# First layer's weighted sums: rows by group of 512 edges instead of by step

## The chip, the cores and the metric

One core of a Trainium2 chip runs the whole program. The metric is the device time in microseconds of one execution, as the median of several runs.

## What is computed

The reference is a stack of four graph layers on 6,250 nodes and 206,250 edges, which arrive sorted by their target node `dst`. Each layer's result is added to `x` and normalised. The change touches the first layer alone, an attention layer with 8 heads of 16 columns:

```
e   = leaky(score_src[src] + score_dst[dst] + edge_bias)      # one number per edge and head
p   = exp(e - max over the edges with the same dst)
msg = x_heads[src] * edge_gate                                # 128 numbers per edge
out = segment_sum(msg * p, dst) / segment_sum(p, dst)         # per node and head
```

The last line is the part at issue: per node, the sum over its edges of the 128-wide row times the edge's weight, and the sum of the weights.

## The kernel before

The program runs its stages one after the other, with a barrier between two stages. Earlier stages have written the gated rows `x_heads[src] * edge_gate` to HBM (`gated`) and hold the weights `p` in `e_score`. `stage_aggregate` (L811) then makes the two segment sums, and `stage_update` divides and normalises.

Edges lie in tiles of 128, four tiles make a group (G = 4, 512 edges), and there are GE = 403 groups. Nodes lie in 49 blocks of 128. Since edges are sorted by node, a group touches one block or a few; the stage runs over pairs of a group and a block in order, called steps: KE = 451 steps, 48 more than groups. The table `steps_e`, made on the device by `stage_steps` (L282), says for step k which group (row 0) and which block (row 1) it has; its row 2 is the group modulo 8 (SLOTS), its row 3 the number of steps that are through when a group is through. Rows 2 and 3 are used by a later stage, `stage_move`, too.

In each step, in rings of R = 8 buffers:

- SyncE loads the group's gated rows into `ag_buf` (L831), 256 KB.
- GpSimd multiplies them by the weights into columns 0 to 127 of `ag_wrow` (L835), and ScalarE copies the 8 weights of each edge into the 8 columns behind them (L898). Both may write a buffer when TensorE is through with the step 8 back (`s_mm`).
- VectorE makes the one-hot matrix `ag_oh`, 128 edges by 128 nodes for each of the four tiles, by comparing a count with the keys (L872, SCALAR_TENSOR_TENSOR).
- TensorE multiplies one-hot by weighted rows, four float32 matmuls that add up in one of four PSUM tiles (L912). Each float32 matmul stands in the trace as two.
- VectorE adds the PSUM tile to the block's rows of `acc` (L885, TENSOR_TENSOR), three steps later.

Every engine works through its own list of instructions in order. `pipeline` (L159) writes the loops: 8 steps in a turn of the loop, so that buffer numbers are constants, and a few steps ahead and behind it written out.

Of the kernel before, what the change touches and what calls it, by code (L numbers as in the profile page):

```python
# [19 lines left out]
ALU = mybir.AluOpType  # L20
# [5 lines left out]
ds = bass.ds  # L26

P = 128
C = 128
# [6 lines left out]
G = 4  # L36
# [11 lines left out]
SLOTS = 8  # L48
# [134 lines left out]
def later(item, by=RING):  # L183

    return not isinstance(item, int) or item >= by
# [13 lines left out]
def flat(ap):  # L199
    return ap.rearrange("p a c -> p (a c)")  # L200

def stage_node_table(nc, v, name, rhs, table, scores, loads=(), kept=W):

    R = 4
    s_x, s_t, s_xt, s_h, s_row, s_sc = (v.sem(f"{name}_{n}") for n in ("x", "t", "xt", "h", "row", "sc"))
    s_st = [v.sem(f"{name}_st{u}") for u in range(R)]
    with ExitStack() as mem:  # L210
# [152 lines left out]
def step_value(nc, eng, steps, row, k, top):  # L363

    _, values = nc.values_load_multi_w_load_instructions(  # L365
        steps[0:1, row, ds(k, 1)], engines=[eng.engine], min_val=0, max_val=top, skip_runtime_bounds_check_because=SURE)
    return values[0]
# [443 lines left out]
def stage_aggregate(nc, v, name, rows, keys, steps, n_steps, groups, weights, heads, acc):  # L811

    R = 8
    s_z, s_ld, s_oh = v.sem(name + "_z"), [v.sem(f"{name}_ld{u}") for u in range(R)], v.sem(name + "_oh")
    s_w, s_wc, s_mm, s_add = v.sem(name + "_w"), v.sem(name + "_wc"), v.sem(name + "_mm"), v.sem(name + "_add")
    s_up = v.sem(name + "_up")
    width = C + heads
    with ExitStack() as mem:
        sb = lambda n, sh, d=F32: mem.enter_context(nc.sbuf_tensor(name + n, sh, d))  # L820
        buf = sb("_buf", [P, R, G, C])
        oh = sb("_oh", [P, R, G, P])
        wrow = sb("_wrow", [P, R, G, width])
        ps = [mem.enter_context(nc.psum_tensor(f"{name}_ps{u}", [P, 512], F32)) for u in range(4)]
        count_up = mem.enter_context(nc.psum_tensor(name + "_up", [P, 512], F32))
        src = rows.rearrange("(t p) c -> p t c", p=P)
        with nc.Block() as block:
            def load(queue, k, u, g):
                if later(k, R):
                    queue.wait_ge(s_w, k - R + 1)  # L830
                queue.dma_start(buf[:, u, :, :], src[:, ds(g * G, G), 0:C]).then_inc(s_ld[u], 16)  # L831

            def weigh(engine, queue, k, u, use, g):
                queue.wait_ge(s_ld[u], use * 16 + 16)
                engine.tensor_tensor(  # L835
                    wrow[:, u, :, 0:C].rearrange("p t (h c) -> p t h c", h=heads),
                    buf[:, u, :, :].rearrange("p t (h c) -> p t h c", h=heads),
                    weights[:, ds(g * G, G), 0:heads][:, :, :, None].broadcast_to([P, G, heads, C // heads]),
                    ALU.mult).then_inc(s_w, 1)

            @block.sync
            def _(sp):
                def loads(k, u, use):
                    g = step_value(nc, sp, steps, 0, k, groups - 1)
                    load(sp, k, u, g)

                pipeline(sp, n_steps, (loads, 0), ring=R)

            @block.gpsimd  # L850
            def _(pool):
                def weighted(k, u, use):
                    g = step_value(nc, pool, steps, 0, k, groups - 1)
                    if later(k, R):
                        pool.wait_ge(s_mm, k - R + 1)
                    weigh(nc.gpsimd, pool, k, u, use, g)

                pipeline(pool, n_steps, (weighted, 0), ring=R)

            @block.vector  # L860
            def _(dve):
                nc.vector.memset(acc[:, :, 0:width], 0.0).then_inc(s_z, 1)
                nc.vector.tensor_copy(count_up[:, 0:P], v.iota[:, :]).then_inc(s_up, 1)
                dve.wait_ge(s_up, 1)

                blocks = Blocks(nc, dve, steps, groups, 3, R)

                def prepare(k, u, use):
                    g, b = blocks.load(k, u)
                    if later(k, R):  # L870
                        dve.wait_ge(s_mm, k - R + 1)
                    nc.vector.scalar_tensor_tensor(  # L872
                        oh[:, u, :, :], count_up[:, None, 0:P].broadcast_to([P, G, P]), v.blk[:, ds(b, 1)],
                        keys[:, ds(g * G, G), None].broadcast_to([P, G, P]), ALU.add,
                        ALU.is_equal).then_inc(s_oh, 1)

                def add(k, u, use):
                    b = blocks.again(k, u)
                    dve.wait_ge(s_mm, k + 1)
                    if later(k, 1):  # L880
                        dve.wait_ge(s_add, k)
                    else:
                        dve.wait_ge(s_z, 1)
                    here = flat(acc[:, ds(b, 1), 0:width])
                    nc.vector.tensor_tensor(here, here, ps[u % 4][:, 0:width], ALU.add).then_inc(s_add, 1)  # L885

                pipeline(dve, n_steps, (prepare, 0), (add, 3), ring=R)

            @block.scalar
            def _(act):  # L890
                nc.scalar.preload_act_table(ACT.Copy)

                def put(k, u, use):
                    g = step_value(nc, act, steps, 0, k, groups - 1)
                    if later(k, R):
                        act.wait_ge(s_mm, k - R + 1)
                        act.wait_ge(s_z, 1)
                    nc.scalar.activation(wrow[:, u, :, C:width], weights[:, ds(g * G, G), 0:heads],  # L898
                                         ACT.Copy).then_inc(s_wc, 1)

                pipeline(act, n_steps, (put, 0), ring=R)

            @block.tensor
            def _(pe):
                def sums(k, u, use):
                    pe.wait_ge(s_oh, k + 1)
                    pe.wait_ge(s_w, k + 1)
                    pe.wait_ge(s_wc, k + 1)
                    if later(k, 4):
                        pe.wait_ge(s_add, k - 3)  # L910
                    for j in range(G):
                        last = nc.tensor.matmul(ps[u % 4][:, 0:width], oh[:, u, j, :], wrow[:, u, j, 0:width],  # L912
                                                start=(j == 0), stop=(j == G - 1))
                    last.then_inc(s_mm, 1)

                pipeline(pe, n_steps, (sums, 0), ring=R)
# [1438 lines left out]
```

## Time and profile before

| what | value |
| --- | --- |
| median of 3 runs | 9192.17 us |
| the runs | 9183.11 to 9197.33 us |
| the profiled execution, first to last instruction | 9188.8 us |
| mean granted TensorE clock | 0.886 |
| the stage that is changed | 2574 to 3141 us of the span |

The profile is one execution, the median is over three others. What lies around the span isn't given by itself; the span is 3.4 us under the median and within the spread of the runs. Engines work beside each other, so busy times don't add up to the span. An engine's sequencer isn't counted as busy.

### The profile page before, as it was taken

The numbers are of one execution on the slowest core, as the hardware profiler recorded it, in microseconds if no ns is written. First come the engines' busy times: TensorE is split into PE (matmuls) and PEld (weight loads), VectorE is DVE, ScalarE is ACT, GpSimd is POOL, SyncE is SP. The second block draws the span as 40 slices with busy tenths as digits, with TensorE's granted clock in tenths as the row PEclk, the third lists the DMA queues.
The fourth block names the chain that finished last, engine by engine and source line by source line (L and its number), as shares of the span: only waits on it lengthen the run. The fifth ranks groups of instructions, "written<-read, shape, count | busy, mean of one in ns | idle before, by whom it ended". The sixth has DMA issues, their size and how long they took to land. (4 is left out here: it accounts for less than half of the span.)

```text
span 9188.8 us, 193747 instructions
## 1 busy us (share of the span) xinstructions
PE 6564.0 (71%) x41828; PEld 5489.2 (60%) x41829; DVE 6345.2 (69%) x11929; ACT 1632.9 (18%) x4649; POOL 6369.9 (69%) x7772
## 2 busy tenths in 40 slices
PE   5999999999378548777777625999768850037752
PEld 3878877888267536666666524777558740026652
DVE  3444444444577868777777524888768899999965
ACT  1111111110221134444444200111410000011100
POOL 2777777775068557777777764888367778877774
PEclk9999999999789879999999857999889975569975
DMA  3777777777067436666666769999359963359974
GB/s 115 207 206 208 208 207 206 209 207 200 24 177 210 128 113 211 209 208 209 209 209 208 213 172 157 273 270 270 103 163 264 259 188 86 87 159 256 253 210 115
DMA packets 2113959, 1742.97 MB, mean 190 GB/s; under 512 B 376688, under 2 KB 1838118, under 8 KB 2113686
## 3 DMA queue, kind: packets, MB, share of 16 engines
q1 hardware_dynamic: 1217548, 819.30, 30.4%
q10 hardware_dynamic: 710140, 472.87, 20.6%
q0 software_dynamic: 186160, 449.72, 17.3%
q14 instruction: 90, 0.74, 0.0%
q8 instruction: 21, 0.34, 0.0%
HBM read 1289.62 MB, written 453.29 MB: 190 GB/s over the span
## 5 line engine op out<-in xcount | busy, mean ns | idle before, releaser
L1592 POOL DMA_INDIRECT z_xg<-table,srci x1664 | 1819.1, 1093 | 512.9 <-issue 466.3
L1162 POOL DMA_INDIRECT sorted<-m_rows,srci x1612 | 1609.0, 998 | 532.4 <-issue 436.1
L464 POOL DMA_INDIRECT g_xg<-table,srci x1612 | 1582.1, 981 | 491.2 <-issue 464.3
L1458 PE MATMUL n_ps<-n_row,n_oh 128*128 128x257 f32 x3712 | 881.2, 389 | 216.0 <-DVE n_row L1434 198.1
L483 PE MATMUL g_psg<-g_wg,g_eT 128*128 128x136 f32 x3224 | 1027.6, 474 | 0.0
L1458 PEld LDWEIGHTS n_ps<-n_row,n_oh 128*128 128x128 f32 x3712 | 677.6, 190 | 419.5 <-issue 337.4
L500 PE MATMUL g_psx<-scores,g_hot 128*128 x3608 | 835.5, 362 | 70.3 <-DVE e_score L591 68.0
L483 PEld LDWEIGHTS g_psg<-g_wg,g_eT 128*128 128x128 f32 x3224 | 769.3, 324 | 191.0 <-issue 191.0
L500 PEld LDWEIGHTS g_psx<-scores,g_hot 128*128 128x128 f32 x3608 | 806.8, 329 | 86.9 <-issue 85.9
L1656 PE MATMUL z_ps<-z_wrow,z_oh 128*128 128x132 f32 x3712 | 603.4, 315 | 329.8 <-issue 188.8
L564 DVE TENSOR_TENSOR g_y<-g_gate,g_xg 128x512 f32<-128x512 f32 x403 | 279.7, 694 | 787.5 <-DMA g_xg<-table,srci 786.8
L835 POOL TENSOR_TENSOR ag_wrow<-ag_buf,e_score 128x512 f32<-128x512 f32 x451 | 467.3, 1057 | 438.8 <-DMA ag_buf<-gated 350.0
L1656 PEld LDWEIGHTS z_ps<-z_wrow,z_oh 128*128 128x128 f32 x3712 | 521.5, 216 | 411.5 <-issue 374.4
L1221 PE MATMUL m_psx<-held,m_hot 128*128 x3608 | 599.1, 316 | 192.8 <-DVE m_rows L1340 120.1
L1221 PEld LDWEIGHTS m_psx<-held,m_hot 128*128 128x128 f32 x3608 | 507.5, 217 | 253.4 <-issue 252.5
L1628 PE MATMUL z_ps<-z_tab,z_ohlo 128*128 128x200 bf16 x4992 | 600.7, 250 | 75.9 <-DVE z_e L1746 71.6
L1340 DVE SCALAR_TENSOR_TENSOR m_rows<-m_rows,follows,m_psx 128x516 f32 x451 | 339.4, 753 | 347.1 <-ACT m_rows L1266 287.3
L523 ACT ACTIVATE g_gate<-g_psg 128x512 f32<-128x512 f32 x403 | 240.6, 597 | 1833.4 <-PE g_psg L483 1752.9
L912 PE MATMUL ag_ps<-ag_wrow,ag_oh 128*128 128x136 f32 x3608 | 489.4, 289 | 80.9 <-DVE ag_oh L872 80.8
L1211 PE MATMUL m_psl<-m_cnt,m_oht 128*128 128x100 f32 x3224 | 542.9, 296 | 0.0
L912 PEld LDWEIGHTS ag_ps<-ag_wrow,ag_oh 128*128 128x128 f32 x3608 | 445.1, 190 | 125.2 <-issue 114.1
L1211 PEld LDWEIGHTS m_psl<-m_cnt,m_oht 128*128 128x128 f32 x3224 | 510.7, 200 | 1.2
(411 smaller groups left out, 12549.7 us busy)
## 6 DMA issues: line engine op xcount, KB each, us to landing
n_row<-sorted SPq DMA_DIRECT2D x464, 520.0 KB, 4.4
z_buf<-gathered ACTq DMA_DIRECT2D x464, 256.0 KB
g_keys<-dst_row ACTq DMA_DIRECT2D x451, 256.0 KB
ag_buf<-gated SPq DMA_DIRECT2D x451, 256.0 KB, 3.2
m_keys<-dst_row ACTq DMA_DIRECT2D x451, 256.0 KB
gathered<-z_xg SPq DMA_DIRECT2D x416, 256.0 KB
gated<-g_y SPq DMA_DIRECT2D x403, 256.0 KB
g_eT<-in_attr_t SPq DMA_DIRECT2D x402, 256.0 KB
```

What stands on the lines that cost most here:

```text
L464: nc.gpsimd.indirect_dma_start(out=xg[:, u, j, :], out_offset=None, in_=v.table[:, :], in_offset=bass.IndirectOffsetOnAxis(ap=v.srci[:, t: ...
L483: last = nc.tensor.matmul(psg[u % 2][:, h, j * W:(j + 1) * W], eT[:, u, (h * H + j) * P:(h * H + j + 1) * P], wg[:, :], start=False, stop= ...
L500: last = nc.tensor.matmul(psx[u % 2][:, j * X8:(j + 1) * X8], hot_t[:, u, j * P:(j + 1) * P], flat(v.scores[:, ds(b, 1), :]), start=True, ...
L835: engine.tensor_tensor(wrow[:, u, :, 0:C].rearrange("p t (h c) -> p t h c", h=heads), buf[:, u, :, :].rearrange("p t (h c) -> p t h c", h= ...
L912: last = nc.tensor.matmul(ps[u % 4][:, 0:width], oh[:, u, j, :], wrow[:, u, j, 0:width], start=(j == 0), stop=(j == G - 1))
L1162: nc.gpsimd.indirect_dma_start(out=v.sorted[:, :], out_offset=bass.IndirectOffsetOnAxis(ap=place[:, t:t + 1], axis=0), in_=rows[:, u, j, : ...
L1211: nc.tensor.matmul(to, oht[:, u, j * P:(j + 1) * P], before, start=True, stop=False)
L1221: last = nc.tensor.matmul(psx[u % 2][:, j // 2, (j % 2) * WH:(j % 2 + 1) * WH], hot_t[:, u, j * P:(j + 1) * P], flat(held[:, ds(b, 1), :]) ...
L1458: last = nc.tensor.matmul(ps[u % 4][:, 0:ROW], oh[:, u, j, :], row[:, u, j, 0:ROW], start=(j == 0), stop=(j == G - 1))
L1592: nc.gpsimd.indirect_dma_start(out=xg[:, u, j, :], out_offset=None, in_=v.table[:, :], in_offset=bass.IndirectOffsetOnAxis(ap=v.dsti[:, t: ...
L1628: nc.tensor.matmul(to, ohlo[:, u, edges], tab[:, n, :, :], start=(n == 0), stop=False)
L1656: last = nc.tensor.matmul(bank[u % 4 // 2][:, u % 2, 0:width], oh[:, u, j, :], wrow[:, u, j, 0:width], start=(j == 0), stop=(j == G - 1))
```

## The change

The steps stay, and so do VectorE's part and the order of the matmuls. SyncE, GpSimd and ScalarE now go over the 403 groups instead of the 451 steps. Group g has slot g modulo 8 in `ag_buf` and `ag_wrow`. SyncE may load group g when TensorE is through with the last step of group g - 8; it reads the number of that step from row 3 of the table and waits for the count `s_mm`. GpSimd and ScalarE wait for the load alone. TensorE has to find the slot: for each step it loads the group (row 0, with the bounds check, for the waits `s_w` and `s_wc`, which count groups now) and the slot (row 2), and the second operand of each matmul has an address worked out from the slot.

```diff
--- before.py
+++ after.py
@@ -811,7 +811,7 @@
 def stage_aggregate(nc, v, name, rows, keys, steps, n_steps, groups, weights, heads, acc):
 
 
-    R = 8
+    R = SLOTS
     s_z, s_ld, s_oh = v.sem(name + "_z"), [v.sem(f"{name}_ld{u}") for u in range(R)], v.sem(name + "_oh")
     s_w, s_wc, s_mm, s_add = v.sem(name + "_w"), v.sem(name + "_wc"), v.sem(name + "_mm"), v.sem(name + "_add")
     s_up = v.sem(name + "_up")
@@ -825,37 +825,27 @@
         count_up = mem.enter_context(nc.psum_tensor(name + "_up", [P, 512], F32))
         src = rows.rearrange("(t p) c -> p t c", p=P)
         with nc.Block() as block:
-            def load(queue, k, u, g):
-                if later(k, R):
-                    queue.wait_ge(s_w, k - R + 1)
-                queue.dma_start(buf[:, u, :, :], src[:, ds(g * G, G), 0:C]).then_inc(s_ld[u], 16)
-
-            def weigh(engine, queue, k, u, use, g):
-                queue.wait_ge(s_ld[u], use * 16 + 16)
-                engine.tensor_tensor(
-                    wrow[:, u, :, 0:C].rearrange("p t (h c) -> p t h c", h=heads),
-                    buf[:, u, :, :].rearrange("p t (h c) -> p t h c", h=heads),
-                    weights[:, ds(g * G, G), 0:heads][:, :, :, None].broadcast_to([P, G, heads, C // heads]),
-                    ALU.mult).then_inc(s_w, 1)
-
-
             @block.sync
             def _(sp):
-                def loads(k, u, use):
-                    g = step_value(nc, sp, steps, 0, k, groups - 1)
-                    load(sp, k, u, g)
-
-                pipeline(sp, n_steps, (loads, 0), ring=R)
+                def load(g, u, use):
+                    if later(g, R):
+                        done = sp.value_load(steps[0:1, 3, ds(g - R, 1)], min_val=1, max_val=n_steps)
+                        sp.wait_ge(s_mm, done)
+                    sp.dma_start(buf[:, u, :, :], src[:, ds(g * G, G), 0:C]).then_inc(s_ld[u], 16)
+
+                pipeline(sp, groups, (load, 0), ring=R)
 
             @block.gpsimd
             def _(pool):
-                def weighted(k, u, use):
-                    g = step_value(nc, pool, steps, 0, k, groups - 1)
-                    if later(k, R):
-                        pool.wait_ge(s_mm, k - R + 1)
-                    weigh(nc.gpsimd, pool, k, u, use, g)
-
-                pipeline(pool, n_steps, (weighted, 0), ring=R)
+                def weighted(g, u, use):
+                    pool.wait_ge(s_ld[u], use * 16 + 16)
+                    nc.gpsimd.tensor_tensor(
+                        wrow[:, u, :, 0:C].rearrange("p t (h c) -> p t h c", h=heads),
+                        buf[:, u, :, :].rearrange("p t (h c) -> p t h c", h=heads),
+                        weights[:, ds(g * G, G), 0:heads][:, :, :, None].broadcast_to([P, G, heads, C // heads]),
+                        ALU.mult).then_inc(s_w, 1)
+
+                pipeline(pool, groups, (weighted, 0), ring=R)
 
             @block.vector
             def _(dve):
@@ -890,26 +880,26 @@
             def _(act):
                 nc.scalar.preload_act_table(ACT.Copy)
 
-                def put(k, u, use):
-                    g = step_value(nc, act, steps, 0, k, groups - 1)
-                    if later(k, R):
-                        act.wait_ge(s_mm, k - R + 1)
-                        act.wait_ge(s_z, 1)
+                def put(g, u, use):
+                    act.wait_ge(s_ld[u], use * 16 + 16)
                     nc.scalar.activation(wrow[:, u, :, C:width], weights[:, ds(g * G, G), 0:heads],
                                          ACT.Copy).then_inc(s_wc, 1)
 
-                pipeline(act, n_steps, (put, 0), ring=R)
+                pipeline(act, groups, (put, 0), ring=R)
 
             @block.tensor
             def _(pe):
                 def sums(k, u, use):
+                    g = pe.value_load(steps[0:1, 0, ds(k, 1)], min_val=0, max_val=groups - 1)
+                    slot = step_value(nc, pe, steps, 2, k, R - 1)
                     pe.wait_ge(s_oh, k + 1)
-                    pe.wait_ge(s_w, k + 1)
-                    pe.wait_ge(s_wc, k + 1)
+                    pe.wait_ge(s_w, g + 1)
+                    pe.wait_ge(s_wc, g + 1)
                     if later(k, 4):
                         pe.wait_ge(s_add, k - 3)
                     for j in range(G):
-                        last = nc.tensor.matmul(ps[u % 4][:, 0:width], oh[:, u, j, :], wrow[:, u, j, 0:width],
+                        last = nc.tensor.matmul(ps[u % 4][:, 0:width], oh[:, u, j, :],
+                                                flat(wrow[:, ds(slot, 1), j, 0:width]),
                                                 start=(j == 0), stop=(j == G - 1))
                     last.then_inc(s_mm, 1)
 

```

What TensorE's list holds in the loop, for a step, is first shown as it was. The rows are TensorE's, from the head of the loop over steps (L170 is the loop's own branch and register work) to its first step's end; `ag_ps` is the PSUM tile, `ag_wrow` and `ag_oh` the operands:

```order
L170 UNCONDITIONAL_BRANCH
L170 ISA
L910 REGISTER_ALU [waits ag0_wc,ag0_w,ag0_oh]
L912 MATMUL ag_ps<-ag_wrow,ag_oh 128x136 [waits ag0_add]
L912 MATMUL ag_ps<-ag_wrow,ag_oh 128x136 x3
L906 REGISTER_ALU
```

A wait by itself isn't shown as a row; it is named at the next one. The same place now, a step within the loop on TensorE:

```order
L893 ISA
L893 TENSOR_LOAD steps_e
L893 ISA x2
L365 ISA
L365 TENSOR_LOAD steps_e
L895 REGISTER_ALU
L896 REGISTER_ALU [waits ag0_oh]
L899 REGISTER_ALU [waits ag0_wc,ag0_w]
L901 ISA [waits ag0_add]
L901 MATMUL ag_ps<-ag_wrow,ag_oh 128x136
L901 ISA
L901 MATMUL ag_ps<-ag_wrow,ag_oh 128x136
```

The last two rows come twice more. The second of the L893 `ISA x2` is the SEQ_ASSERT, every other ISA row is a FUSED_REGOPS. So a step had two register instructions and one wait beside its four matmuls, and now has two value loads, six FUSED_REGOPS and one more with the bounds, one SEQ_ASSERT, three REGISTER_ALU and one wait, and no two matmuls follow each other directly.

SyncE's list in the loop, before, for one load:

```order
L365 ISA
L365 TENSOR_LOAD steps_e
L830 REGISTER_ALU
L831 ISA [waits ag0_w]
L831 DMA ag_buf<-gated 128x4x128
```

and now:

```order
L832 ISA
L832 TENSOR_LOAD steps_e
L832 ISA x2
L834 ISA [waits ag0_mm]
L834 DMA ag_buf<-gated 128x4x128
```

The value load stays and reads another row of the table, its bounds are checked, and the wait is for TensorE's count and no longer for GpSimd's.

## Rows read from the trace of the kernel before

**Rows 1.** The page of the profile, its first line.

```profile
span 9188.8 us, 193747 instructions
```

**Rows 2.** Busy time of each engine by stretch; columns are named in the first row.

```profile
core 0: us, PE busy (x) PEld busy (x) DVE busy (x) ACT busy (x) POOL busy (x), PEclk, DMA share, GB/s
...
2700.00:2800.00 100.00, 86.61 (x642) 78.59 (x640) 77.93 (x162) 18.53 (x81) 83.11 (x82) 1.00 0.72 211
```

**Rows 3.** Groups by line in the stage, 2575 to 3141 us: busy, mean | idle before.

```profile
L912 PE MATMUL ag_ps<-ag_wrow,ag_oh 128*128 128x136 f32 x3608 | 489.4, 289 | 80.9 <-DVE ag_oh L872 80.8
L835 POOL TENSOR_TENSOR ag_wrow<-ag_buf,e_score 128x512 f32<-128x512 f32 x451 | 467.3, 1057 | 438.8 <-DMA ag_buf<-gated 350.0 <-PE ag_ps L912 88.4
...
L872 DVE SCALAR_TENSOR_TENSOR ag_oh<-ag_up,blk,keys 128x512 f32<-128x512 f32 x451 | 338.2, 750 | 124.4 <-issue 93.5 <-PE ag_ps L912 22.3 <-DVE ag_up L863 0.5
L885 DVE TENSOR_TENSOR acc<-acc,ag_ps 128x136 f32 x451 | 129.6, 287 | 1.3 <-DVE acc L885 0.7 <-PE ag_ps L912 0.6
```

**Rows 4.** Instructions in order of time, VectorE, two steps that follow: start, duration.

```profile
2809.13 0.75 DVE L872 SCALAR_TENSOR_TENSOR ag_oh<-ag_up,blk,keys 128x512 f32<-128x512 f32 x1 [0.55 <-issue]
...
2810.69 0.75 DVE L872 SCALAR_TENSOR_TENSOR ag_oh<-ag_up,blk,keys 128x512 f32<-128x512 f32 x1 [0.55 <-issue]
```

**Rows 5.** VectorE's sequencer, 2600 to 3100 us, L365: ns min/median/max.

```profile
L365 DVEq TENSOR_LOAD <-steps_e x554: 298/303/325, 2600.2 to 3100.0; - x185
L365 DVEq FUSED_REGOPS  x504: 57/57/57, 2600.1 to 3099.9; - x168
```

**Rows 6.** The same for L872, and then L881.

```profile
L872 DVEq ALU_OP  x402: 40/40/40, 2600.0 to 3099.1; - x134
...
L872 DVEq FUSED_REGOPS  x401: 186/186/186, 2601.4 to 3098.9; - x134
...
L881 DVEq EVENT_SEMAPHORE  x396: 21/21/21, 2582.6 to 3140.1; - x198
```

**Rows 7.** Instructions in order of time, TensorE, 2800 to 2806 us.

```profile
2801.63 1.19 PE L912 MATMUL ag_ps<-ag_wrow,ag_oh 128*128 128x136 f32 x8 [0.37 <-DVE ag_oh L872]
...
2803.12 3.10 PE L912 MATMUL ag_ps<-ag_wrow,ag_oh 128*128 128x136 f32 x24 [0.30 <-DVE ag_oh L872]
```

**Rows 8.** TensorE's sequencer, L365, then L170 and L908: ns min/median/max.

```profile
L365 PEldq TENSOR_LOAD <-steps_e x902: 296/303/1221, 164.7 to 5418.3; - x181
...
L365 PEldq FUSED_REGOPS  x853: 46/46/51, 199.5 to 5404.7; - x171
...
L170 PEldq FUSED_REGOPS  x511: 44/50/73, 47.8 to 9067.1; - x171
...
L170 PEldq ALU_OP  x511: 32/32/32, 54.1 to 9104.1; - x171
L170 PEldq COMPARE_BRANCH  x511: 76/208/226, 54.2 to 9104.2; - x171
...
L908 PEldq EVENT_SEMAPHORE  x451: 51/51/3432, 2572.1 to 3137.6; - x151
```

**Rows 9.** ScalarE's sequencer at L1261, a value load with its bounds: ns.

```profile
L1261 ACTq FUSED_REGOPS  x495: 42/152/172, 3366.5 to 5427.2; - x165
...
L1261 ACTq SEQ_ASSERT  x451: 18/18/23, 3366.7 to 5427.4; - x151
```

**Rows 10.** Weight loads in order of time, the move stage, 4402 us.

```profile
4402.42 0.24 PEld L1179 LDWEIGHTS m_pst<-m_ident,m_ohlo 128*128 128x128 bf16 x4
...
4403.23 0.97 PEld L1221 LDWEIGHTS m_psx<-held,m_hot 128*128 128x128 f32 x8 [0.31 <-issue]
```

**Rows 11.** In order of time: the stage's first weight loads and its last addition.

```profile
2579.25 2.99 PEld L912 LDWEIGHTS ag_ps<-ag_wrow,ag_oh 128*128 128x128 f32 x13 [9.77 <-DVE ag_oh L872]
...
3140.27 0.29 DVE L885 TENSOR_TENSOR acc<-acc,ag_ps 128x136 f32 x1 [0.25 <-DVE acc L885]
```

**Rows 12.** Transfers into ag_buf, from issue to landing.

```profile
DMA to landing us min/median/max: 2.6/3.2/5.3
```

## The prediction

> **What bounds the stage now.** The page gives the span, 9188.8 us [rows 1]. The stage runs from its first weight load at 2579.25 to the end of its last addition, 3140.27 + 0.29 = 3140.56 [rows 11]: 561.3 us for 451 steps, 1.245 us a step. What lies before and after is separated from it by barriers, so only this stretch can change.
>
> The view by stretch, read next, names no engine as full: in a steady 100 us TensorE is busy 86.61, GpSimd 83.11, VectorE 77.93 us [rows 2]. The groups by line say more. GpSimd's multiplication takes 1.057 us; apart from the one wait for the first data, what it waits for is TensorE (88.4 us), which frees its buffers. TensorE in turn waits for VectorE's one-hots (80.8 us), and nowhere in that row for GpSimd. VectorE's one-hot instruction waits most for "issue", 93.5 us: for nothing that another engine does [rows 3].
>
> The order of time shows what that is. Two one-hots that follow each other start at 2809.13 and 2810.69, 1.56 us apart, and between them the engine has work for 0.75 + 0.29 us only, with a pause of 0.55 before the second [rows 3, 4]. VectorE's sequencer is busy then. The slow steps have two value loads: 2 x 0.303, three address computations at 0.057, one for the one-hot at 0.186, three additions at 0.040 and a wait at 0.021, together 1.10 us [rows 5, 6]. The other 0.46 us, over these ten instructions and the two that are handed on, is 0.038 us at each hand-over. So a sequencer's instructions add up one behind another with a gap between them, and where their sum exceeds the engine's work, it is the step. Here three steps in eight have two value loads and are slow; the other five have one.
>
> TensorE has room: a step alone takes 1.19 us from first matmul to last end, three back to back 3.10, 1.03 each [rows 7].
>
> **What is removed.** 48 loads, 48 multiplications and 48 copies, 451 down to 403, and the value load and address work ahead of each multiplication and copy. GpSimd loses 48 x 1.057 = 51 us of work. That is worth nothing as long as GpSimd waits for TensorE [rows 3], and it does all the more if TensorE gets slower.
>
> **SyncE's new wait.** It waits for TensorE to be through with the group eight back, no longer for GpSimd. Behind the waiting instruction stands only the next load. A transfer lands 3.2 us after issue, 5.3 at most [rows 12], then comes 1.057 us of multiplication: at most 6.4 us in a ring that takes eight groups, at least 8 x 1.245 = 10 us, to turn. Nothing is late. I cost it at nothing; with no cover it would be about one landing, 5 us, a ring turn.
>
> **TensorE's sequencer.** This is the term that counts. The prices, in us:
>
> - two value loads, 2 x 0.303 = 0.606 [rows 8]
> - the bounds, which TensorE doesn't compute anywhere in this trace. The same three comparisons take 0.152 on ScalarE and the assertion 0.018 [rows 9]. TensorE's ordinary FUSED_REGOPS take 0.046 as ScalarE's short ones do about, so I take ScalarE's 0.152. Bounds: 0.046 below, VectorE's dearest such instruction, 0.186, above [rows 6, 8]
> - six FUSED_REGOPS for addresses, one of them two operations long: 6 x 0.046 = 0.276 [rows 8]
> - three REGISTER_ALU, 3 x 0.032 = 0.096, and a wait, 0.051 when nothing is waited for [rows 8]
>
> Together 1.20 us in 14 instructions. Then the gaps. In the move stage TensorE's weight loads show one: matmuls begin at 4402.42, the next ones, behind a single value load, at 4403.23, with a pause of 0.31 "issue" [rows 10]. Between these two moments its sequencer hands on eight matmuls and does two FUSED_REGOPS, a value load, an addition and a wait, 2 x 0.046 + 0.303 + 0.032 + 0.051 = 0.478. That leaves 0.33 of the 0.81 us: I take 0.058 for each of the five gaps and the last 0.04 for handing on the matmuls, so about 0.02 for a matmul that stands between two register instructions. A step has 14 x 0.058 = 0.81 us of gaps and 4 x 0.02 = 0.08 of matmuls. Step: 1.20 + 0.81 + 0.08 = 2.09 us.
>
> The turn of the loop, once in eight steps, adds an addition (0.032), a branch (0.208) and two gaps (0.116): 0.36 us or 0.045 a step; its FUSED_REGOPS takes the place of one in the step, at about the same price [rows 8]. So 2.135 us a step in the 440 steps of the loop. The 11 that are written out have constants for indices and need two FUSED_REGOPS and two additions less: 2.09 - 2 x 0.104 - 2 x 0.09 = 1.70.
>
> Is this hidden? The four matmuls of a step take 1.03 to 1.19 us and now run while the sequencer works on; but then the array is out of work and the next step isn't handed on yet. TensorE's work of 1.03 lies beside the 2.135, not on top of it. The gap that VectorE left is filled in the same way: its 1.245 a step is under 2.135, so its one-hots will be early, up to eight steps, and what it waits for is TensorE's sums. Next late after that is nobody: GpSimd has 403 x 1.057 us in a stage of 940.
>
> Sum: 440 x 2.135 + 11 x 1.70 = 958 us, less 1.2 for the first step's value loads, which lie before the first one-hot is there, and with 0.7 for the last matmuls' end and the last addition: 957.5 against 561.3, so **+396 us**. Against the profiled execution: 9188.8 + 396 = 9585. The median of the runs is 3.4 us over that span, so 9192.2 + 396 = **9588 us**.
>
> **The clock.** TensorE would be busy 1.03 of 2.135 us. In the steady stretch the granted clock is 1.00 [rows 2]; at the stage's start, behind 9.77 us of idleness, 13 weight loads take 2.99 us, 0.23 each [rows 11], the lower of the two levels (1.2 GHz), against 0.12 later. Should the clock stay at that level through the stage, a step's eight would take 8 x 0.23 = 1.84 us, still under 2.135. So a lower clock costs nothing here, and it is a bound that stands close behind.
>
> **A page against the row.** My value load costs 0.303 us, from the row. The Trainium skill, "DMA: Bandwidth & Descriptors", section on latency and other measured facts, gives a `tensor_load` a floor of about 600 ns. No row of this trace supports it for a load from SBUF. By the page's figure the sum would be 451 x 2 x 0.3 = 271 us more, an estimate of 9859; the row decides.
>
> **Rivals.**
>
> *Hidden, no change (9192 us).* Value loads could go beside queued matmuls, with TensorE's sequencer always far enough ahead. For: the value load at 4402 was made while matmuls ran. Against: the same place shows the array standing still for 0.31 us behind one load [rows 10], VectorE's slow steps show the same [rows 4], and an average of 2.1 us can't be kept ahead of 1.245. Chance 0.04. The Trainium skill, "Advanced Engine Details and Errata", section on the sequencer and instruction queues, says that further engine instructions can be read and queued while the microcode runs a control instruction. By that rule this rival would be the forecast; it would hold the step at 1.245. The two pauses just named speak against it.
>
> *Faster (9132 us).* If GpSimd's pace, multiplication plus its value load, set the step and VectorE only seemed to, 48 steps fewer would save 48 x 1.245 = 60 us. The place is GpSimd's line in the loop, and it decides if TensorE ever waits for `ag_wrow`. The rows show no such wait [rows 3]. Chance 0.03.
>
> *A smaller loss.* If register instructions between matmuls had VectorE's gap, 0.038, and the bounds cost 0.046: a step is shorter by 14 x 0.02 + 0.106 = 0.39 us, 451 times is 174 us, so 9414. With the bounds alone, 48 us less: 9540. Partial overlap would fall in the same region. Chance under 9530: 0.08.
>
> *A larger loss.* If each of the four matmuls costs a whole gap (0.038 more each): 451 x 4 x 0.038 = 69 us, 9657; with the bounds at 0.186, 15 more, 9672. If the value load had to wait until the matmuls of the step before are done, the 1.03 us would come on top, +465: 10,050. The load at 4402 comes right behind matmuls that are only begun, with no room for such a wait. Chance over 9660: 0.09, nearly all of it near 9670.
>
> **How the numbers follow.** The main case, TensorE's sequencer at 2.0 to 2.3 us a step, has 0.76. Range 9530 to 9660, from the bounds above. No change within 0.2% (18 us, about what the measurement can tell) 0.04, faster 0.03, slower 0.93.
>
> **What would show it.** In the profile after: the stage 940 to 970 us long; steps of TensorE 2.1 us apart; its matmuls and weight loads waiting for "issue", about 1 us a step; the value load at 0.30 twice a step, the bounds at 0.15; VectorE's one-hots or additions waiting for `ag_ps`; GpSimd waiting for loads that wait for TensorE; nothing else in the program changed. Wrong would be: TensorE waiting for one-hots still, or a step shorter than 2.0 us though the sequencer's durations are as said, which would mean that it overlaps with itself.

## The result

The changed kernel takes 9582.11 us (median of 4 runs, 9573.99 to 9587.46) against 9192.66 us before (four runs; three of them gave the 9192.17 that the forecast starts from): the ratio is 1.0423, 95% interval 1.0409 to 1.0438. That is 389 us more; forecast were 396 and 9588 us.

The first line of the changed kernel's page, and the first weight load and the last addition of the stage in the order of time:

```profile
span 9578.6 us, 194948 instructions
```

```profile
2575.35 6.28 PEld L901 LDWEIGHTS ag_ps<-ag_wrow,ag_oh 128*128 128x128 f32 x32 [10.06 <-issue]
...
3525.01 0.30 DVE L875 TENSOR_TENSOR acc<-acc,ag_ps 128x136 f32 x1 [1.56 <-PE ag_ps L901]
```

The stage lasts from 2575.35 to 3525.31, 950.0 us, against 561.3 [rows 11]: 388.6 us more, and the whole span grew by 389.8 [rows 1]. All of the difference lies in this stage. A step takes 950.0 / 451 = 2.106 us.

Busy time by stretch, for the changed kernel, the columns as before:

```profile
core 0: us, PE busy (x) PEld busy (x) DVE busy (x) ACT busy (x) POOL busy (x), PEclk, DMA share, GB/s
...
2700.00:2800.00 100.00, 66.46 (x381) 56.88 (x382) 48.87 (x94) 9.63 (x42) 44.55 (x43) 0.88 0.38 110
...
3400.00:3500.00 100.00, 67.62 (x382) 57.59 (x382) 49.40 (x96) 9.86 (x43) 44.96 (x43) 0.86 0.39 111
```

TensorE's busy time in 100 us is down from 86.61 to about 67 us, with fewer matmuls and a granted clock of 0.86 to 0.88 instead of 1.00 [rows 2]. GpSimd fell from 83 to 45. In every stretch of 100 us of the stage the clock lay between 0.85 and 0.91. No engine is full, and each is less so than before.

The groups by line over the stage (busy, mean ns | idle before, and what ended it):

```profile
L901 PE MATMUL ag_ps<-ag_wrow,ag_oh 128*128 x3608 | 636.4, 330 | 323.0 <-DVE acc L875 217.8 <-ACT ag_wrow L885 52.1 <-POOL ag_wrow L842 41.2
L901 PEld LDWEIGHTS ag_ps<-ag_wrow,ag_oh 128*128 128x128 f32 x3608 | 542.9, 224 | 416.5 <-issue 416.4
L842 POOL TENSOR_TENSOR ag_wrow<-ag_buf,e_score 128x512 f32<-128x512 f32 x403 | 426.2, 1058 | 863.5 <-DMA ag_buf<-gated 863.5
L862 DVE SCALAR_TENSOR_TENSOR ag_oh<-ag_up,blk,keys 128x512 f32<-128x512 f32 x451 | 338.3, 751 | 242.9 <-issue 241.5 <-PE ag_ps L901 0.9 <-DVE ag_up L853 0.5
L875 DVE TENSOR_TENSOR acc<-acc,ag_ps 128x136 f32 x451 | 133.1, 295 | 240.3 <-PE ag_ps L901 238.2
```

Here is the reader's trap. The row of the matmuls says that TensorE waited 217.8 us for VectorE's additions. The row of the weight loads below it, which come first in each matmul, says 416.4 us of "issue", for nothing that another engine does. VectorE's additions in turn waited 238.2 us for TensorE. GpSimd waited 863.5 us for transfers, but that takes in the time before the first data; from 2575 us on it is 515.4, and those transfers wait for TensorE:

```profile
L842 POOL TENSOR_TENSOR ag_wrow<-ag_buf,e_score 128x512 f32<-128x512 f32 x399 | 422.1, 1058 | 515.5 <-DMA ag_buf<-gated 515.4
```

Here the name of an engine behind a matmul's idle time is only the last signal that came before it. The order of time shows the same:

```profile
3000.40 0.99 PEld L901 LDWEIGHTS ag_ps<-ag_wrow,ag_oh 128*128 128x128 f32 x8 [1.18 <-issue]
...
3001.74 0.30 DVE L875 TENSOR_TENSOR acc<-acc,ag_ps 128x136 f32 x1 [0.64 <-PE ag_ps L901]
...
3002.42 0.99 PEld L901 LDWEIGHTS ag_ps<-ag_wrow,ag_oh 128*128 128x128 f32 x8 [1.03 <-issue]
...
3002.51 0.75 DVE L862 SCALAR_TENSOR_TENSOR ag_oh<-ag_up,blk,keys 128x512 f32<-128x512 f32 x1 [0.48 <-issue]
3003.76 0.30 DVE L875 TENSOR_TENSOR acc<-acc,ag_ps 128x136 f32 x1 [0.50 <-PE ag_ps L901]
3004.46 0.99 PEld L901 LDWEIGHTS ag_ps<-ag_wrow,ag_oh 128*128 128x128 f32 x8 [1.04 <-issue]
```

Weight loads start at 3000.40, 3002.42 and 3004.46, 2.02 and 2.04 us apart, for 0.99 us of work. The addition at 3001.74 ends at 3002.04, 0.38 us before the loads of 3002.42 begin, and these name only issue; what holds them is TensorE's own sequencer. Its work, the value load of the group with its bounds (L893), the address computations of the matmuls (L901), and what stands at L899 (ns, min/median/max):

```profile
L893 PEldq FUSED_REGOPS  x836: 42/151/168, 2566.8 to 3522.6; - x168
L893 PEldq TENSOR_LOAD <-steps_e x451: 295/304/322, 2566.4 to 3522.2; - x151
L893 PEldq SEQ_ASSERT  x451: 18/18/32, 2567.0 to 3522.8; - x151
```

```profile
L901 PEldq FUSED_REGOPS  x1804: 46/46/46, 2575.3 to 3523.9; - x181
```

```profile
L899 PEldq EVENT_SEMAPHORE  x282: 51/51/51, 2582.1 to 3523.5; - x141
L899 PEldq ALU_OP  x165: 32/32/32, 2589.6 to 3507.7; - x165
```

The value load takes 0.304 us; the comparison takes 0.151, which is what was borrowed from ScalarE [rows 9]; the assertion 0.018; an address 0.046.

Added up record by record from the trace, the work of TensorE's sequencer in the stage makes 542 us of durations and 407 us of gaps between one and the next, 949 of the stage's 950 us. The median gap is 0.058 us behind a value load, 0.061 behind an addition and 0.078 where a matmul is handed on in between; none is more than 0.16 us wider than these. So there is hardly room in the stage in which TensorE's sequencer waits for another engine.

### The profile page after: what moved, and what is told of

Same layout as the page of the kernel before. It is cut to its first block and busy times, and to the rows that moved or that the text cites. A ratio compares the mean times of both kernels' runs of the same rounds, so it can differ in the third digit from the quotient of the medians.

```text
span 9578.6 us, 194948 instructions
## 1 busy us (share of the span) xinstructions
PE 6710.9 (70%) x41828; PEld 5592.4 (58%) x41829; DVE 6375.3 (67%) x11929; ACT 1622.9 (17%) x4601; POOL 6324.8 (66%) x7723
## 5 line engine op out<-in xcount | busy, mean ns | idle before, releaser
L464 POOL DMA_INDIRECT g_xg<-table,srci x1612 | 1578.6, 979 | 491.0 <-issue 468.5
L842 POOL TENSOR_TENSOR ag_wrow<-ag_buf,e_score 128x512 f32<-128x512 f32 x403 | 426.2, 1058 | 863.5 <-DMA ag_buf<-gated 863.5
L901 PE MATMUL ag_ps<-ag_wrow,ag_oh 128*128 x3608 | 636.4, 330 | 323.0 <-DVE acc L875 217.8
L901 PEld LDWEIGHTS ag_ps<-ag_wrow,ag_oh 128*128 128x128 f32 x3608 | 542.9, 224 | 416.5 <-issue 416.4
L1646 PEld LDWEIGHTS z_ps<-z_wrow,z_oh 128*128 128x128 f32 x3712 | 511.8, 212 | 416.4 <-issue 384.1
```

Source lines behind the costliest of these rows:

```text
L464: nc.gpsimd.indirect_dma_start(out=xg[:, u, j, :], out_offset=None, in_=v.table[:, :], in_offset=bass.IndirectOffsetOnAxis(ap=v.srci[:, t: ...
L842: nc.gpsimd.tensor_tensor(wrow[:, u, :, 0:C].rearrange("p t (h c) -> p t h c", h=heads), buf[:, u, :, :].rearrange("p t (h c) -> p t h c", ...
L1646: last = nc.tensor.matmul(bank[u % 4 // 2][:, u % 2, 0:width], oh[:, u, j, :], wrow[:, u, j, 0:width], start=(j == 0), stop=(j == G - 1))
```

## The experiments

The theory is that TensorE's sequencer sets the step: each register instruction and value load adds its own time and a gap of 0.058 us, one behind the other, and matmuls run beside it. The first rival is that the loads are late, since SyncE waits for TensorE now and GpSimd was found waiting for transfers. The second is that matmuls whose operand's address comes from a register are slow, or that the fallen clock makes the step. "The stage" below is measured as above, from the first weight load to the end of the last addition.

| kernel | stage, us | us a step | whole program, us (before beside it) |
| --- | --- | --- | --- |
| before | 561.3 | 1.245 | 9192.66 |
| after | 950.0 | 2.106 | 9582.11 (9192.66) |
| e1, no bounds check | 822.9 | 1.825 | 9462.92 (9190.85) |
| e2, one value load | 663.4 | 1.471 | 9297.93 (9190.85) |
| e3, old prefetch | 949.8 | 2.106 | 9586.88 (9190.85) |
| e4, before, two value loads | 807.9 | 1.791 | 9443.41 (9190.85) |
| e5, before, one value load | 561.2 | 1.244 | 11037.83 (11033.84) |
| e6, before, address from registers | 561.2 | 1.244 | 11028.07 (11033.84) |
| e7, before, VectorE's turn of 16 | 513.7 | 1.139 | 10978.81 (11033.84) |
| e8, after, three value loads | 1204.8 | 2.671 | 11700.13 (11038.73) |
| e9, e2 and VectorE's turn of 16 | 662.8 | 1.470 | 11142.29 (11038.73) |
| e10, e7 again | 513.7 | 1.139 | 10989.14 (11038.73) |

e5 to e7 ran on another chip and e8 to e10 on a third; on these two the kernel before takes 11034 and 11039 us. They are spoken of at the end. Compare each with the number beside it.

**e1_unchecked.** `loose_value` is a value load without the check whose result goes through a maximum with 0:

```diff
-                    g = pe.value_load(steps[0:1, 0, ds(k, 1)], min_val=0, max_val=groups - 1)
+                    g = loose_value(nc, pe, steps, 0, k, groups - 1)
```

> The changed kernel, with TensorE's value load of the group made without the bounds check (the wait value is kept positive by a max in its place). Theory, TensorE's sequencer sets the step: the comparison (0.151 us), the assertion (0.018) and their two gaps (0.116) go, 0.285 us a step, so 451 x 0.28 = 126 us less than the changed kernel: 9456 us. Rival one, the loads into ag_buf are late since SyncE waits for TensorE: no change, 9582. Rival two, matmuls with an address from a register, or the lower granted clock, make the step: no change, 9582.

The stage lost 127.0 us, where 126 had been forecast (0.285 x 451 = 128.5, unrounded; the maximum, which the expectation gave no price, makes the 0.032 us addition for the wait an instruction of 0.042); the program took 9462.92 us. Two sequencer instructions that touch neither data nor transfers are worth a third of the loss, so neither rival explains it.

**e2_one_load.**

```diff
-                    g = pe.value_load(steps[0:1, 0, ds(k, 1)], min_val=0, max_val=groups - 1)
-                    slot = step_value(nc, pe, steps, 2, k, R - 1)
+                    g = loose_value(nc, pe, steps, 0, k, groups - 1)
+                    slot = nc.s_assert_within(g & (R - 1), 0, R - 1, skip_runtime_bounds_check_because=SURE)
```

> The changed kernel, with one value load on TensorE instead of two and no bounds check: the slot is the group's three low bits, worked out in a register. Theory: by the prices of the trace the step's sequencer work falls from 2.11 to about 1.46 us, 0.65 x 451 = 293 us: 9289 us; VectorE's 1.245 is then close below. Rivals (late loads; register addresses or clock): no change, 9582.

9297.93 us; the stage lost 286.5 us, 293 had been forecast. The groups by line show TensorE still pausing for issue and VectorE hardly waiting for sums any more:

```profile
L909 PEld LDWEIGHTS ag_ps<-ag_wrow,ag_oh 128*128 128x128 f32 x3608 | 450.1, 190 | 222.8 <-issue 222.7
...
L909 PE MATMUL ag_ps<-ag_wrow,ag_oh 128*128 x3608 | 537.3, 292 | 135.6 <-POOL ag_wrow L850 50.8 <-ACT ag_wrow L893 33.4 <-issue 28.4
...
L883 DVE TENSOR_TENSOR acc<-acc,ag_ps 128x136 f32 x451 | 130.9, 290 | 4.2 <-PE ag_ps L909 4.2
```

It keeps all that the change was to save, 403 transfers and multiplications, and is still 107 us slower than before.

**e3_old_prefetch.** SyncE waits for GpSimd again, and GpSimd and ScalarE for TensorE:

```diff
-                        done = sp.value_load(steps[0:1, 3, ds(g - R, 1)], min_val=1, max_val=n_steps)
-                        sp.wait_ge(s_mm, done)
+                        sp.wait_ge(s_w, g - R + 1)
...
+                    if later(g, R):
+                        pool.wait_ge(s_mm, loose_value(nc, pool, steps, 3, g - R, n_steps))
                     pool.wait_ge(s_ld[u], use * 16 + 16)
...
-                    act.wait_ge(s_ld[u], use * 16 + 16)
+                    if later(g, R):
+                        act.wait_ge(s_mm, loose_value(nc, act, steps, 3, g - R, n_steps))
```

> The changed kernel, with the loads let go as before: SyncE waits for GpSimd's count, GpSimd and ScalarE wait for TensorE (by a value load of their own, without a check), all still once per group. TensorE's list is the same. Theory: no change against the changed kernel, 9582 within 10 us. Rival one, late loads: a good part of the 390 us comes back, under 9400.

9586.88 us, and a stage within 0.2 us of the changed kernel's. TensorE's weight loads and GpSimd's multiplications:

```profile
L911 PEld LDWEIGHTS ag_ps<-ag_wrow,ag_oh 128*128 128x128 f32 x3608 | 544.3, 224 | 414.9 <-issue 414.7
L851 POOL TENSOR_TENSOR ag_wrow<-ag_buf,e_score 128x512 f32<-128x512 f32 x403 | 425.6, 1057 | 859.8 <-PE ag_ps L911 512.1 <-DMA ag_buf<-gated 346.5 <-issue 0.2
```

TensorE pauses for the same 415 us of issue. GpSimd's idle time is the same 860 us too, only that 512.1 of it now stands against TensorE and 346.5, once, before the first data. Letting the transfers go by the old rule changes nothing; the first rival falls.

**e4_before_two_loads.** The kernel before, with what TensorE's list got and nothing else; both new waits ask for less than the two behind them, since a step's group and slot are never larger than its number:

```diff
+                    g = pe.value_load(steps[0:1, 0, ds(k, 1)], min_val=0, max_val=groups - 1)
+                    slot = loose_value(nc, pe, steps, 2, k, R - 1)
                     pe.wait_ge(s_oh, k + 1)
+                    pe.wait_ge(s_w, g + 1)
+                    pe.wait_ge(s_wc, slot + 1)
```

> The kernel before, loads, multiplications and matmul addresses untouched, with TensorE alone making two value loads a step, one with the bounds check, whose values serve in waits that are always met. Theory: its sequencer work becomes about 1.80 us a step against VectorE's 1.245, so 0.555 x 451 = 250 us more than before: 9442 us. Rivals (late loads; register addresses): no change against before, 9192, since neither is in it. If value loads were hidden behind matmuls: 9192 too.

9443.41 us; the stage, by these two rows, 807.9 us, 246.6 more than before against 250 forecast. The third row is busy time in a stretch, where the clock is 1.00:

```profile
2578.45 3.67 PEld L924 LDWEIGHTS ag_ps<-ag_wrow,ag_oh 128*128 128x128 f32 x16 [10.03 <-issue]
...
3386.06 0.30 DVE L893 TENSOR_TENSOR acc<-acc,ag_ps 128x136 f32 x1 [1.12 <-PE ag_ps L924]
```

```profile
3000.00:3100.00 100.00, 64.98 (x444) 55.02 (x444) 57.72 (x112) 12.85 (x56) 58.95 (x56) 1.00 0.50 145
```

With every transfer and every address as before and the clock at its upper level, the loss is there. The second rival is left only what e6 would show.

**e5_before_one_load.**

```diff
+                    g = loose_value(nc, pe, steps, 0, k, groups - 1)
                     pe.wait_ge(s_oh, k + 1)
+                    pe.wait_ge(s_w, g + 1)
```

> The kernel before, with one value load a step on TensorE, without a check, whose value serves in a wait that is always met. Theory: TensorE's sequencer has about 0.93 us of work a step, under VectorE's 1.245: no change, 9192 within 18 us. Rival, a value load stops the array or waits until its matmuls are done, so that each one costs its 0.36 us or more: 451 x 0.36 = 162 us, 9355 or above.

The ratio to before is 0.9997 (0.9987 to 1.0007). The stage, in two rows, is 561.2 us:

```profile
3172.14 3.00 PEld L922 LDWEIGHTS ag_ps<-ag_wrow,ag_oh 128*128 128x128 f32 x13 [9.95 <-POOL ag_wrow L843]
...
3733.02 0.30 DVE L893 TENSOR_TENSOR acc<-acc,ag_ps 128x136 f32 x1 [0.40 <-PE ag_ps L922]
```

One value load costs nothing while TensorE's sequencer has some 0.94 us of work (e4's 1.791 less the second load at 0.565, from e8 below, and the check at 0.285) under VectorE's 1.245. So a value load neither stops the array nor waits for it: with its 0.36 us on top of the matmuls' 1.03 a step would be 1.39. What counts is on which side of the slowest engine the sum comes out.

**e6_before_register_slot.** `zero` is a value load ahead of the loop, of step 0's group, which is 0:

```diff
+                    here = nc.s_assert_within((zero + k) & (R - 1), 0, R - 1, skip_runtime_bounds_check_because=SURE)
                     for j in range(G):
-                        last = nc.tensor.matmul(ps[u % 4][:, 0:width], oh[:, u, j, :], wrow[:, u, j, 0:width],
+                        last = nc.tensor.matmul(ps[u % 4][:, 0:width], oh[:, u, j, :],
+                                                flat(wrow[:, ds(here, 1), j, 0:width]),
```

> The kernel before, with the slot of the matmuls' second operand worked out in registers from the step's number (it comes out as the same constant), an address computation ahead of each matmul, no value load in the loop. Theory: 1.03 us of sequencer work a step, under 1.245: no change, 9192 within 18 us. Rival, that a matmul with an address from a register, or matmuls that don't follow each other directly, are slow by themselves: over 9250.

The ratio is 0.9997 (0.9984 to 1.0009), the stage 561.2 us. An address computation ahead of each matmul is free in this place too, and the matmuls themselves take 292 ns on average for 289 before. The second rival falls, as far as addresses and interrupted matmuls go.

**e7_vector_turn_16 and e10_vector_turn_16_again.** This asks what bound the stage before:

```diff
-                blocks = Blocks(nc, dve, steps, groups, 3, R)
+                blocks = Blocks(nc, dve, steps, groups, 3, 2 * R)
...
-                        oh[:, u, :, :], count_up[:, None, 0:P].broadcast_to([P, G, P]), v.blk[:, ds(b, 1)],
+                        oh[:, u % R, :, :], count_up[:, None, 0:P].broadcast_to([P, G, P]), v.blk[:, ds(b, 1)],
...
-                pipeline(dve, n_steps, (prepare, 0), (add, 3), ring=R)
+                pipeline(dve, n_steps, (prepare, 0), (add, 3), ring=2 * R)
```

> The kernel before, with VectorE's loop 16 steps long instead of 8 (buffers as before): three of 16 steps have a second value load instead of three of 8, and the loop turns half as often. Theory, VectorE's sequencer is what bound the stage before: a step falls from 1.245 to about 1.12 us, 451 x 0.127 = 57 us less: 9135 us. If GpSimd, with 1.057 us of work and its own gaps, comes to bind first, less is gained: 9135 to 9165. If VectorE was not the bound: no change, 9192.

> The kernel of e7_vector_turn_16 once more beside the others, since it ran on a chip on which the kernel before took 11034 us. Theory: the stage takes the same 48 to 57 us less whatever the rest of the program takes: 9135 to 9144 where the kernel before takes 9192. If the gain belonged to that chip: no change.

The ratios are 0.9951 (0.9939 to 0.9962) and 0.9956 (0.9943 to 0.9969): faster than the kernel before beside them, by 55 and 50 us. The stage is 47.6 us shorter in both than the 561.3 of the kernel before. VectorE's one-hots in e7, in order of time, and the stage's ends:

```profile
3401.55 0.75 DVE L872 SCALAR_TENSOR_TENSOR ag_oh<-ag_up,blk,keys 128x512 f32<-128x512 f32 x1
...
3402.65 0.75 DVE L872 SCALAR_TENSOR_TENSOR ag_oh<-ag_up,blk,keys 128x512 f32<-128x512 f32 x1 [0.15 <-PE ag_ps L912]
...
3405.61 0.75 DVE L872 SCALAR_TENSOR_TENSOR ag_oh<-ag_up,blk,keys 128x512 f32<-128x512 f32 x1
...
3407.06 0.75 DVE L872 SCALAR_TENSOR_TENSOR ag_oh<-ag_up,blk,keys 128x512 f32<-128x512 f32 x1 [0.50 <-PE ag_ps L912]
...
3408.64 0.75 DVE L872 SCALAR_TENSOR_TENSOR ag_oh<-ag_up,blk,keys 128x512 f32<-128x512 f32 x1 [0.55 <-issue]
...
3410.21 0.75 DVE L872 SCALAR_TENSOR_TENSOR ag_oh<-ag_up,blk,keys 128x512 f32<-128x512 f32 x1 [0.56 <-issue]
...
3411.70 0.75 DVE L872 SCALAR_TENSOR_TENSOR ag_oh<-ag_up,blk,keys 128x512 f32<-128x512 f32 x1 [0.54 <-issue]
...
3412.70 0.75 DVE L872 SCALAR_TENSOR_TENSOR ag_oh<-ag_up,blk,keys 128x512 f32<-128x512 f32 x1
...
3419.62 0.75 DVE L872 SCALAR_TENSOR_TENSOR ag_oh<-ag_up,blk,keys 128x512 f32<-128x512 f32 x1
```

```profile
3168.88 6.29 PEld L912 LDWEIGHTS ag_ps<-ag_wrow,ag_oh 128*128 128x128 f32 x31 [9.77 <-DVE ag_oh L872]
...
3682.27 0.29 DVE L885 TENSOR_TENSOR acc<-acc,ag_ps 128x136 f32 x1 [0.25 <-DVE acc L885]
```

The steps with two value loads, here 1.58, 1.57 and 1.49 us from one start to the next, come three times in sixteen. Once in sixteen comes a step of 1.45 at the turn of the loop: the row at 3407.06 names TensorE, but VectorE's sequencer is at the loop's branch just before. One more, whose row names TensorE too, takes 1.10; the others take 0.98 to 1.00, which is VectorE's own work. So it was VectorE that bound the stage before, in the slow steps by its sequencer. GpSimd, the other candidate in the expectation, still waits 45.6 us for TensorE. The step is 1.139 us, where 1.12 was worked out: 9 us less gained than forecast. A turn takes 18.07 us, 1.129 a step, and the 32 steps that are written out ahead of the longer loop take 1.25 each; that makes up most of the 9 us, though no run tried it.

**e8_third_load.**

```diff
                     slot = step_value(nc, pe, steps, 2, k, R - 1)
+                    b = loose_value(nc, pe, steps, 1, k, NBX - 1)
                     pe.wait_ge(s_oh, k + 1)
+                    pe.wait_ge(s_oh, b + 1)
```

> The changed kernel with a third value load a step on TensorE (the block, without a check, its value in a wait that is always met). Theory: by the same prices the load with its address, the computation of the wait's value and the gaps add 0.565 us a step, 451 x 0.565 = 255 us: 9837 us where the kernel before takes 9192. Rivals (late loads, register addresses, clock): no change against the changed kernel.

The expectation's 9837 holds where the kernel before takes 9192 us. Here the kernel took 11700.13 us, 661 over the kernel before; less the 389 of the change that is 272, 17 more than the stage shows; about 14 of these lie behind the stage, by the profiles of e9 and e10 on the same chip, and why is not known. The stage, by its two ends, is 1204.8 us, 254.8 more than the changed kernel's, and 255 were forecast:

```profile
3177.30 1.86 PEld L911 LDWEIGHTS ag_ps<-ag_wrow,ag_oh 128*128 128x128 f32 x8 [10.17 <-issue]
...
4381.77 0.29 DVE L883 TENSOR_TENSOR acc<-acc,ag_ps 128x136 f32 x1 [1.92 <-PE ag_ps L911]
```

The stretch 3300 to 3400 us of the same kernel:

```profile
3300.00:3400.00 100.00, 73.87 (x299) 63.51 (x300) 38.52 (x75) 7.61 (x34) 34.99 (x34) 0.61 0.30 86
```

The granted clock is 0.61, near its lower level (1.2 GHz), and the sum by the sequencer's prices still comes out to the microsecond. That was the last thing the second rival had: a step's eight weight loads at the lower level take 1.84 us [rows 11], under 2.67.

**e9_one_load_turn_16.** The edits of e2 and e7 together.

> The kernel with one value load on TensorE (e2_one_load), with VectorE's loop 16 steps long. Theory: TensorE's sequencer, 1.46 us a step, binds here and not VectorE: as e2_one_load within 15 us, 9298 where the kernel before takes 9191. If VectorE still bound, about 55 us less, 9243.

103.6 us over the kernel before, where e2 was 107.1; the stages are 662.8 and 663.4 us. The edit that took 48 us from the stage of the kernel before helps nothing where TensorE's sequencer binds.

## Why the prediction was right

**What bounds it.** VectorE's sequencer, said the prediction, by two value loads in three steps of eight. e7 confirmed it by taking away half of the second loads. One step in eight, at the loop's turn, is slow as well, 1.36 us in the trace of the kernel before; the prediction didn't name it. The hand-over of 0.038 us at VectorE was not tested by itself; in order of time most of the gaps there are 0.035 to 0.048.

**What is removed** was worth nothing, as forecast: e3 and e4 differ in whether transfers and multiplications run 403 or 451 times, and both times the stage is what TensorE's list makes it. No run takes the 48 away and leaves TensorE's list as short as it was, so that they would be worth nothing under a step of 1.245 us too is argued from GpSimd's waits [rows 3] and not shown.

**SyncE's wait** costs nothing: e3.

**TensorE's sequencer.** The price list held: value load 0.303 forecast and 0.304 measured, comparison 0.152 and 0.151, assertion 0.018 and 0.018, address 0.046 and 0.046. The gap of 0.058 us, and 0.02 for a matmul between two instructions, came from one pause of 0.31 us in another stage, which alone can't give two values: how it was shared out was a choice. The medians in the stage, 0.058 and 0.078, bear both out, and so do e1 (127.0 us for 126) and e8 (254.8 for 255). The forecast for the stage was 957.5 us, and it took 950.0. The term that was mis-sized is "three REGISTER_ALU, 3 x 0.032": it was read from the first step of the loop. The rows at L899 above show an addition 165 times and a plain wait 282 times, that is, in 3 steps of 8 and in 5 of 8; in those five the value that is waited for had been worked out already. An addition and its gap are 0.09 us, and the 275 of them that the loop doesn't have are 25 us. The stage was only 7.5 us under the forecast, because the gaps took 17 us more than 0.058 and 0.078 each would give: 359 of some 6100 are over 0.02 us wider and hold 13.6 of the 17. Why these are wider is open. Two errors of opposite sign made the forecast closer than its terms. Counting the instructions over a whole turn of the loop would have cost nothing.

**Hidden?** The matmuls' 1.03 to 1.19 us did lie beside the sequencer's 2.11, and e5 shows the whole case: a value load is free up to the other engines' pace.

**The clock** fell as was allowed for, to 0.85 to 0.91, and cost nothing: in e8 it was 0.60 to 0.67 and the step still came to its price.

**The page against the row.** The value load took 0.304 us and, in e8, a third one with its address, wait and gaps 0.565 us. The Trainium skill, "DMA: Bandwidth & Descriptors", section on latency and other measured facts, has a floor of about 600 ns for a `tensor_load`; no load of this stage shows it, and by it the changed kernel would have come to an estimate of 9859 us. The Trainium skill, "Advanced Engine Details and Errata", section on the sequencer and instruction queues, says that further engine instructions can be read and queued while the microcode runs a control instruction. e5 agrees as far as the array goes: a value load a step there changes nothing, ratio 0.9997. But in this stage the control instructions don't overlap with each other (542 us of work and 407 of gaps in 950), and once their sum is the step, queued matmuls hide none of it.

The rivals "hidden", "faster" and "a larger loss" didn't come, and the smaller loss neither.

## What to carry to other kernels

Count an engine's register instructions, waits and value loads in a loop as work: durations plus a gap for each, and compare the sum with the step of the slowest engine, not with the engine's own busy share. This change made the work on the data smaller by 11% and lost, because TensorE's sequencer came to 0.86 us a step more than VectorE's pace. When a stage is bound by such a sum, a load without its check or one load where there were two is worth what the list says (e1, e2), and what was tried on other engines was worth nothing (e3, e9). A longer turn of the loop pays only on the engine that binds (e7 against e9).

## What was not expected

What goes with a lower clock can be read across the runs. With matmuls that follow each other directly and a step of 1.79 us, e4 had 1.00; the changed kernel, with an address computation between matmuls and 2.11 us, had 0.85 to 0.91. Other runs take the two apart. First e6, whose step is 1.24 us, then e1, whose step is 1.82, both with address computations between the matmuls:

```profile
3300.00:3400.00 100.00, 88.79 (x647) 79.94 (x646) 78.00 (x162) 18.57 (x81) 83.72 (x82) 1.00 0.72 211
```

```profile
2900.00:3000.00 100.00, 67.84 (x440) 57.42 (x440) 56.83 (x110) 11.24 (x49) 51.36 (x49) 0.97 0.44 128
```

So the computations in between don't lower the clock by themselves; with them it fell as the step grew: 1.00 in e6 and in e2 (1.47 us), 0.97 to 0.98 in e1, 0.85 to 0.91 here, 0.60 to 0.67 in e8 (2.67 us). Without them no step over 1.79 us was run, so whether they have a part in it beyond that isn't shown. TensorE's busy time misleads here, since at a lower clock the same work is busy for longer: 67 us for some 380 matmul records in 100 us here, 65 us for 444 in e4.

The chip of e5 to e7 runs the kernel before in 11034 us instead of 9192, while this stage took 561.2 us in e5, whose time is that of the kernel before. The gather's instruction, in the rows below, takes nearly the same time too, 978 and 981 ns. What is slower is seen in the row of what the DMA moved, in 40 equal slices, and in that of the first layer's gather (L464): first both rows of e7, then both of the kernel before where it takes 9192:

```profile
GB/s 111 161 159 161 162 163 162 161 160 162 110 111 232 101 122 150 149 151 149 150 152 152 154 157 144 186 271 270 171 108 190 192 192 133 85 81 209 208 197 115
```

```profile
L464 POOL DMA_INDIRECT g_xg<-table,srci x1612 | 1577.3, 978 | 1080.6 <-DVE g_es L566 609.8 <-issue 470.2 <-DVE g_y L564 0.6
```

```profile
GB/s 115 207 206 208 208 207 206 209 207 200 24 177 210 128 113 211 209 208 209 209 209 208 213 172 157 273 270 270 103 163 264 259 188 86 87 159 256 253 210 115
```

```profile
L464 POOL DMA_INDIRECT g_xg<-table,srci x1612 | 1582.1, 981 | 491.2 <-issue 464.3 <-DVE g_es L566 26.8
```

But GpSimd waits 609.8 us instead of 26.8 for the rows that they bring to be used, and slices that gather move some 160 GB/s instead of 207. This stage began 590 us later in e7 than in the kernel before at 9192, and the 589 us more that the gather's row waits account for it. Where the rest of the 1842 us goes was not followed up, and why the transfers are slower on that chip is not known from these runs. It says how to compare: whole programs only with the kernel before on the same chip, and a stage's own length across chips only where it has been seen to be the same.
